# Diagonal tap weights on GpSimd, halved first projections and an earlier place for two scales in a fused Mamba-2 block

## The reference

```python
x = x + 0.5 * ffn(layernorm(x))        # W = (q - zeros) * scales, plus a rank 16 pair, plus bias
x = x + attn(layernorm(x))             # mamba2 block and a gated MLP
x = x + 0.5 * ffn(layernorm(x))

zxbcdt = rmsnorm(x) @ w_in.T           # z 512, xs 128, Bs 128, Cs 512, dt 4
xBC = silu(conv4(concat(xs, Bs, Cs)) + conv_b)      # causal, depthwise, 4 taps
# scan in chunks of 128 tokens, 4 heads; y = (Yd + Yo + D * xh) * silu(z)
h = x + y @ w_out.T
out = h + (silu(h2 @ gate_w.T) * (h2 @ up_w.T)) @ down_w.T     # h2 = rmsnorm(h), 1792 wide
```

## Time and profile before

| | |
|---|---|
| time, median of 3 | 753.17 us (751.98 to 754.31) |
| time of the profiled execution | 752.58 us |
| its span, first to last instruction | 750.8 us |
| PE busy | 737.4 us (98%) |
| DVE busy | 638.3 us (85%) |
| ACT busy | 456.5 us (61%) |
| POOL busy | 340.9 us (45%) |

### The profile page before, as it was taken

One profiled execution on the slowest core, in us unless ns is written; L12 is line 12 of the kernel. 1 busy time (PEld: TensorE's weight loads), 2 busy tenths in 40 slices (PEclk: granted clock), 3 DMA queues, 4 the chain that ended last, 5 costly groups with the idle time before them and its releaser, 6 DMA issues.

```text
span 750.8 us, 10655 instructions
## 1 busy us (share of the span) xinstructions
PE 737.4 (98%) x3424; PEld 359.9 (48%) x3424; DVE 638.3 (85%) x1257; ACT 456.5 (61%) x895; POOL 340.9 (45%) x391
## 2 busy tenths in 40 slices
PE   8999999999999999979999999999999999999998
PEld 3444455555555565534444444444444444444444
DVE  7799999899989997969899977977977978767994
ACT  4868888787787777435446456456356456444441
POOL 5631455665453357796323243243242242214574
PEclk9999999999999999999999999999999999999999
DMA  8933656574431233440612735634734733434464
GB/s 295 205 74 71 161 109 118 127 141 99 96 88 34 41 75 93 92 105 1 155 28 50 162 56 97 157 56 85 169 57 84 161 65 71 84 71 80 116 169 141
DMA packets 98790, 77.67 MB, mean 103 GB/s; under 512 B 65600, under 2 KB 73088, under 8 KB 98736
## 3 DMA queue, kind: packets, MB, share of 16 engines
q0 software_dynamic: 17280, 31.46, 23.6%
q1 hardware_dynamic: 78592, 41.01, 21.1%
q10 hardware_dynamic: 2864, 4.52, 2.2%
HBM read 24.77 MB, written 5.54 MB: 40 GB/s over the span
## 4 chain that ended last, share of the span: by engine, by line
PE 71%; DVE 17%; POOL 3%; issue 3%; ACT 3%; DMA 2%; ACTq 0%; POOLq 0%; DVEq 0%; SPq 0%
PE PS L2290 62%; DVE stage L1678 2%; DVE st L1500 1%; PE PS L2428 1%; DMA x_t<-hb 1%; PE PS L2420 1%; PE PS L2386 1%; DVE h2n_p L1591 1%; DVE raw L1678 1%; PE PS L2413 1%; PE PS L2404 1%; PE PS L2378 1%; PE PS L2417 1%; PE PS L2396 1%; DVE S L1635 1%
## 5 line engine op out<-in xcount | busy, mean ns | idle before, releaser
L2290 PE MATMUL PS<-h,w_in 128*128 128x512 f16 x480 | 108.1, 379 | 0.4 <-DMA h<-hn_p 0.4
L2290 PE MATMUL PS<-h,x_t 128*128 128x512 f16 x408 | 94.3, 380 | 0.6 <-DVE PS L2114 0.5
L785 POOL DMA_DIRECT2D xs<-x x42 | 36.7, 881 | 92.1 <-ACT x L1363 90.7
L2290 PE MATMUL PS<-n_T,stage 128*128 128x512 f16 x288 | 72.9, 384 | 3.9 <-DVEq L1732 3.9
L2290 PEld LDWEIGHTS PS<-h,w_in 128*128 128x128 f16 x480 | 46.4, 98 | 62.1 <-issue 11.1
L1363 ACT ACTIVATE x<-PS,d_d 128x512 f32<-128x512 f32 x59 | 40.3, 682 | 39.3 <-PE PS L2290 38.4
L2290 PEld LDWEIGHTS PS<-h,x_t 128*128 128x128 f16 x408 | 39.5, 98 | 49.2 <-issue 2.7
L586 POOL TENSOR_TENSOR r<-mv,mhalf 128x1 f32<-128x1 f32 (+1 forms) x32 | 29.1, 908 | 53.1 <-DVE mv L1504 38.4
L1333 ACT ACTIVATE xds<-tm,dgh 128x512 f32<-128x512 f32 x24 | 17.3, 722 | 53.2 <-DVE tm L2214 53.2
L2290 PE MATMUL PS<-pre,stage 128*128 128x512 f16 x192 | 49.3, 379 | 0.0
L2290 PEld LDWEIGHTS PS<-n_T,stage 128*128 128x128 f16 x288 | 28.3, 99 | 38.8 <-DVEq L1732 4.4
(11 more groups left out here) (349 smaller groups left out, 1882.4 us busy)
## 6 DMA issues: line engine op xcount, KB each, us to landing
xs<-x POOLq DMA_DIRECT2D x58, 256.0 KB, 3.3
xs<-n POOLq DMA_DIRECT2D x21, 256.0 KB, 3.3
xl<-x POOLq DMA_DIRECT2D x17, 256.0 KB, 3.3
x_t<-x_in SPq DMA_DIRECT2D x16, 256.0 KB, 3.5
x_t<-hb POOLq DMA_DIRECT2D x16, 256.0 KB, 4.7
out<-x_t SPq DMA_DIRECT2D x15, 256.0 KB, 2.3
raw_gu<-gate_t SPq DMA_DIRECT2D x7, 512.0 KB, 4.5
raw_gu<-up_t SPq DMA_DIRECT2D x7, 512.0 KB, 6.3
```

Of the source, the lines that this page charges most:

```text
L785: po.dma_start(end_row(c), d_tmps[d % 3], accum_op=ALU.add).then_inc(s_acc[d % 3], 16)
L2290: ins = pe.matmul(out_, lhs(a, b, k), rhs(a, b, k), start=first and n == 0, stop=last and n == len(todo) - 1)
```

## The change

At the start: POOL builds the twelve diagonal matrices instead of ACT, two at a time between its other work, and clears `hist`, `state` and `dA` instead of DVE; the first two wait for the loads of `s_head`. The small tables are padded to 32 rows on the host, so their four loads wait for no clearing and stand first in SP's queue; the bias load stands behind the q loads. ACT does `w_in_sum` sooner, `tc0(4)` behind `hi1(2, 2)`, and `w_in_hi` of piece 0 in front of `hi0(5, 1)`. DVE does `w_in_bound`, `max_row(1)` and `both_scales` each one step sooner. PE does projections 0 and 1 in halves of 256 tokens; the first halves stand around `first_t0(5)`, in front of `first_f(5)`. Three idle float32 matmuls are gone, and two of the nine junk ones.

At the end of the scan: DVE does `t_los(0, 1)` behind `gate_up(0, 3)`, and `t_los(1, 2)`, `gate_lo(0, 4)` and `lo2(15)` behind `gate_up(0, 4)` but in front of `scale_read(1)`; POOL does `rms2(15)` four sums sooner; ACT's list follows.

```diff
-N_WARM = 9
+N_WARM = 7
         for q in range(NPL):
-            put_proj(0, q)
+            if q < NPC:
+                PLAN["proj", 0, q] = B_CONV[q], (e_scale, 1)
+            else:
+                put_proj(0, q)
...
+            def build_dw(b, first):
+                for k in range(first, first + NTAP // 2):
+                    last = po.tensor_scalar(dw[:, b, k, :], ident[:, :], cw[:, b, k:k + 1], None, ALU.mult)
+                if first > 0:
+                    last.then_inc(e_dw, 1)
...
+            po.wait_ge(s_head, 48)
+            build_dw(0, 0)
             ln0(0, 0)
+            build_dw(0, 2)
...
             xb(1, 1)
+            build_dw(1, 0)
             ln0(3, 3)
+            build_dw(1, 2)
+            build_dw(2, 0)
             xb(2, 2)
+            build_dw(2, 2)
             ln1_chain(0, 0)
...
-                sums(8, 16)
+                sums(8, 12)
                 rms2(3 * CH + 3, 3)
-                sums(16, 20)
+                sums(12, 20)
...
-                t_his(1, 0, 1, 2, 3)
+                t_his(1, 0, 1)
...
+            gate_a(0, EARLY_GU)
+            t_his(1, 2)
             hi2(NCH - 1, CH - 1)
+            gate_b(0, EARLY_GU)
...
+            t_his(1, 3)
...
-                t_los(0, 1)
                 gate_up(0, 3)
                 residual2(c, 3)
                 gate_lo(0, 3)
-                t_los(0, 2, 3)
+                t_los(0, 1, 2, 3)
                 lo2(c - 1)
                 bound_row(1)
-                t_los(1, 0, 1, 2, 3)
-
+                t_los(1, 0, 1)
...
             gate_up(0, EARLY_GU)
+            t_los(1, 2)
+            gate_lo(0, EARLY_GU)
+            lo2(NCH - 1)
             scale_read(1)
             scales(1)
             descale(1)
-            gate_lo(0, EARLY_GU)
+            t_los(1, 3)
...
+            def proj_half(q, n):
+                b, freed = PLAN["proj", 0, q]
+                at, cols = DI + q * P, slice(n * (ST // 2), (n + 1) * (ST // 2))
...
             first_f(4)
+            proj_half(0, 0)
             first_t0(5)
+            proj_half(1, 0)
             first_f(5)
-            pe.wait_ge(e_zero, 2)
-            for _ in range(3):
-                pe.matmul(bank(B_SS), idle_r[:, 0:P], idle_r[:, :], start=True, stop=True)
```

More of the change, by code:

```diff
@@ L30, in build @@
 def build(nc, x_in, w_in_t, conv_w, conv_b, a_log, d_skip, dt_bias, w_out_t, ln1_w, ln2_w,
-          gate_t, up_t, down_t, q_t, scales_t, zeros_t, lora_a, lora_b_t, bias, out):
+          gate_t, up_t, down_t, q_t, scales_t, zeros_t, lora_a, lora_b_t, bias, out, RANK):
     T, DM = x_in.shape
@@ L640, in _ @@
             po.sem_inc(e_tab, 1)
+            for cleared in (hist[:, :, :], state[:, :, :], dA[:, :, :]):
+                chain(po.memset(cleared, 0.0))
+            po.wait_ge(s_head, 48)
+            build_dw(0, 0)
             ln0(0, 0)
+            build_dw(0, 2)
             chain(po.memset(tri[:, :], 1.0))
@@ L952, in taps_done @@
                 return (e_cv, n + 1) if n < NPC else (e_taps, n + 1 - NPC)
[L954 to L957, removed]
             def conv_pre(b):
@@ L2082, in _ @@
             x1_stats(1, 1, B_P[1])
+            w_in_bound()
             lo1(0, 0)
             prep0(4, 0)
+            max_row(1)
             x1_stats(2, 2, B_P[0])
-            w_in_bound()
             lo1(1, 1)
             prep0(5, 1)
-            max_row(1)
+            both_scales()
             x1_stats(3, 3, B_P[1])
-            both_scales()
             lo1(2, 2)
+            w_in_lo(0)
             lo1(3, 3)
-            w_in_lo(0)
             x1_stats(4, 0, B_P[0])
@@ L2125, in _ @@
             late_steps()
-            lo2(NCH - 1)
             def down(i):
@@ L2315, in proj @@
                 if q == 0:
-                    if i == 0:
-                        for c in range(CH):
-                            pe.wait_ge(s_h1[c], 16)
-                        pe.wait_ge(e_wlo, 1)
-                    else:
-                        pe.wait_ge(s_hT, i * CH * 16)
+                    pe.wait_ge(s_hT, i * CH * 16)
                 if i == 0 and q == CB:
@@ L2325, in proj @@
                 product(bank(b), lambda a, b, k: w_in[b][:, k, at:at + P], lambda a, b, k: h2T[a][:, k, tokens], KB).then_inc(e_proj, 1)
+            def proj_half(q, n):
+                b, freed = PLAN["proj", 0, q]
+                at, cols = DI + q * P, slice(n * (ST // 2), (n + 1) * (ST // 2))
+                if q == 0:
+                    for c in range(n * (CH // 2), (n + 1) * (CH // 2)):
+                        pe.wait_ge(s_h1[c], 16)
+                if n == 0:
+                    pe.wait_ge(e_wlo, 1)
+                    pe.wait_ge(*freed)
+                last = product(PS[:, b, cols], lambda a, b_, k: w_in[b_][:, k, at:at + P], lambda a, b_, k: h2T[a][:, k, cols], KB)
+                if n == 1:
+                    last.then_inc(e_proj, 1)
             def steps(i):
@@ L2734, in columns, with padded @@
         return np.asarray(v).reshape(-1, P).T
+    def padded(rows):
+        return np.concatenate([rows, np.zeros((QUAD - rows.shape[0], rows.shape[1]), rows.dtype)])
     arrays = {
@@ L2760 @@
     out = nc.dram_tensor("out", arrays["x_in"].shape, F32, kind="ExternalOutput").ap()
-    build(nc, out=out, **args)
+    build(nc, out=out, RANK=np.asarray(L0_ffn_lora_A).shape[0], **args)
     r = run_bass_kernel_spmd(nc, [arrays], core_ids=[0])
```

83 lines of the change are left out of this document (32 added, 51 removed).

## The result

The changed kernel took 759.03 us (median of 5, 757.18 to 759.18), the kernel before 754.18 us in the same comparison (5 runs): ratio 1.0064, 95% interval 1.005 to 1.0078. That is slower by 4.8 us, outside the range given. Its profiled execution has a span of 755.6 us, 4.8 more than the 750.8 of before, so the traces hold a difference of the same size. It is one of the two shorter executions (757.39 us at a mean clock of 0.995); the three of 759.0 to 759.2 us had 0.991 to 0.993. PE's busy time barely changed (736.9 us, before 737.4); what grew is its waits, and the stretches at the lower clock.

What follows compares the result with a forecast made beforehand. PE was taken as the bound, busy 737.4 of 750.8 us. Head +0.2 and end of the scan +0.7 gave +0.9: 753.5 us on the profiled execution's 752.58, 754.1 against the median, stated as 753.8, range 749.9 to 755.9.

Steps and rivals of the forecast that it cites:

- The head, +0.2 forecast: Start of the kernel up to `steps(0)`: net 0.2 us slower, with bounds of -1.7 and +1.5.
- So `ln0(0)` ends at 7.1 + 1.4 + 0.9 = 9.4: POOL's start: tap table lands at 7.1, two products take 1.4, `ln0(0)` 0.9, so it ends at 9.4 us.
- PE stands still for some 2 us there: PE ahead of its first transposes: idle some 2 us, transposing at 10.3 instead of 9.21, `first_f(0)` at 14.5.
- the rival of the falling clock: Rival: PE's 3.0 us stall ahead of `first_f(4)` lowers the clock, 1.7 us more, total 756.0 us; chance 0.14.
- the step on `tc0(4)`: Head: `tc0(4)` behind `hi1(2)` ends at 33.95, so `first_f(4)` starts 2.5 us later, PE idle about 3.0 us.
- has the 0.5 us at the mask in hand: Start of the scan: PE, 0.4 us late, can absorb that in its 0.5 us wait for POOL's decay mask.
- What is gained at the head by all engines together stays to the end: Mask to 311 us: PE hardly waits, so a gain at the head by all engines is kept in full.
- the rival in which the head keeps its gain: Rival: POOL's products hide, `steps(0)` comes at 44.7, the head gains 1.7 us, total 751.6 us; chance 0.16.
- The end of the scan, +0.7 forecast: Near 332 us: `e_wscale` comes at 332.8 instead of 332.16, 0.7 us slower, bounds -3.0 and +2.0.
- The bank's 0.5 us: Near 313 us: `gate_up(0, 3)` 0.6 us sooner on DVE removes PE's 0.5 us wait for a bank.
- POOL's wait for `t_los(0, 1)` is 6 us: End of the scan: POOL waits 6 us, before 3.67, for `t_los(0, 1)`; its sum starts at 314.7 instead of 312.08.
- The early scales: Rival: DVE runs unhindered, the 3.9 us scales wait becomes 2.4, clock stays up, 3.0 us saved, total 749.8; chance 0.22.

Runs made afterwards that it cites:

- e1: Changed kernel with its end of the scan written as in the kernel before, head still changed: ratio 1.0035, span 752.0 us.
- e4: Changed kernel with POOL's `ln0(0)` ahead of the tap table's wait and the first two products: ratio 1.0054, span 756.4 us.
- e13: e10 with POOL's second-panel weight sums (`s_adds(1)`) moved ahead of five sums of h2: ratio 0.994, median 748.87 us.
- e15: Head of the kernel before combined with e13's end of the scan: ratio 0.9946, median 748.95 us.
- e5: Changed kernel with PE waiting only for DVE's copy of the bounds out of the bank, not for the scales' end: ratio 1.0058, span 755.6 us.
- e9: e8's head with the end of the scan reordered anew on DVE, ACT and POOL: ratio 0.9984, median 751.40 us.
- e3: Changed kernel with `t_los(0, 1)` alone put back ahead of `gate_up(0, 3)`: ratio 1.0013, span 753.1 us.
- e8: e3 with `ln0(0)` first on POOL, tap products later on POOL, and `tc0(4)` ahead of `hi1(2)`: ratio 0.998, span 750.0 us.
- e6: Changed kernel with ACT's `tc0(4)` put back ahead of `hi1(2)`: ratio 1.0069, span 757.7 us.
- e7: Changed kernel with 16 junk matmuls on PE in the stall ahead of `first_t0(0)`: ratio 1.0062, span 756.3 us.
- e14: Changed kernel with POOL's `s_adds(1)` one sum sooner: ratio 1.0061, span 757.7 us.
- e10: e9 with `both_scales`, `w_in_lo(0)` and `w_in_hi(0)` sooner and `small_scales` behind `w_in_lo(1)` in the head: ratio 0.998, median 752.25 us.

## Why the prediction was wrong

**The head, +0.2 forecast, +2.44 measured.** It comes apart in four. The step that failed is the first, `first_f(0)`: forecast +0.1, measured +2.8. "So `ln0(0)` ends at 7.1 + 1.4 + 0.9 = 9.4" had the table land at 7.1, by the issue-to-landing time of the kernel before, though I wrote that the loads fill the DMA engines and the change puts others in front; it landed at 8.15. The products took 0.60 each, not 0.70. So the transposes came at 11.42, not 10.3, "PE stands still for some 2 us there" became 3.66, and the clock fell: from the transposes to `first_f(0)` it took 5.77 us, and 4.33 in e1, where the clock stayed up. I had the rival of the falling clock, with a price of 1.7 us (here 1.4), but tied it to the stall ahead of `first_f(4)` and did not ask it of this one. Nor did I ask when x would land behind the padded tables; without the table's wait that is what leaves 0.96 us of the stall in e4.

From `first_f(0)` to `first_f(4)`: forecast 19.5 us, measured 18.9, before 17.1. POOL's queue came as forecast (the first bias DMA at 14.90 for 14.4, `ln1_chain(0)` at 24.55 for 24.5), and the step on `tc0(4)` was right. Where the first stall is nearly away (e4) `first_f(4)` starts at 33.92, forecast 33.95, behind 3.31 us of stall, forecast 3.0, and the rival's clock is there as well. That it fits so closely is luck: in e4 `x1_stats(2)` starts at 28.17 and `hi1(2)` 3.7 us behind it, where I had 28.9 and 3.0. And in the changed kernel `x1_stats(2)` starts at 30.35, behind the two waits on ACT's last row sum that I left out.

From `first_f(4)` to `steps(0)`: forecast 12.95, measured 12.67, before 14.82; the halves and the dropped idle matmuls are worth the 2 us that I took. Last, I took off 0.4 us, as PE "has the 0.5 us at the mask in hand". Of the 2.5 us at `steps(0)` 2.44 arrived: POOL's mask came 2.5 us later too (its first select at 88.32, before 85.83), and the wait of 0.5 us stayed.

**"What is gained at the head by all engines together stays to the end"** holds for what is lost. A gain of 1.1 us at `steps(0)` was gone at 304 us (e13 against e15), 0.6 of it in the longer wait for the first masked S, which DVE and POOL brought no sooner. The first 0.7 us did arrive: e15 has the head of the kernel before, but its profiled execution ran `steps(0)` at 45.54 and not at 46.27, and was 0.8 us sooner at 304 us. So the rival in which the head keeps its gain could not have come true as priced.

**The end of the scan, +0.7 forecast, +2.37 measured.** The working up to the scales was near: POOL's sum behind `t_los(0, 1)` started at 317.37, on the old clock 314.93 (forecast 314.7), its wait was 6.5 us (6), and the scales' release came 1.1 us later than before (0.7). The bank's 0.5 us were gained and more was lost to the spread, as `bound_row(1)` stood behind a `t_los` and a `lo2` of 1.64 and 1.75 us beside POOL's sums; both vanish in the wait that DVE ends. The step that failed here is that the sum stopped at `e_wscale`. "POOL's wait for `t_los(0, 1)` is 6 us" stands there without its second consequence: all of POOL's queue, and with it the second panel's sums, come 5.2 us later, 2.8 beyond the head's delay, and PE met them 23 us behind the scales for 1.15 us more. e5, e9 and e13 show that this queue and the last transposition are what this place costs, as much as the scales.

**The sum.** 2.44 + 2.37 = 4.8 us, the difference of the traces. Of the 3.9 us that were missed, 2.2 are the head's (2.7 by the table's landing with the stall and the clock behind it, 0.4 by the mask's wait, less 0.5 and 0.3 at the other two), 0.4 the scales', and 1.3 the second panel's.

**The rivals.** The early scales, with the clock up, came true in e3 and in e8, which has the same end of the scan, and in e3 0.4 us arrived against before of the 3.0 that I had given them. In the changed kernel the wait was 4.0 us. The clock case was the right side and the right mechanism at the wrong stall.

## What to carry to other kernels

When an operation is moved behind a wait, follow the whole queue behind it to its last consumer, not to the next wait that the profile shows: here POOL's sums came due 23 us behind the last wait that I looked at. A wait on a semaphore names what PE stood for, not what would release it if that came sooner: take it away in a trial (e5) before building on it. Where work is moved to an idle engine, its place counts for more than its engine, and the first thing to price is whether its own input is there yet.

## What the runs showed of the hardware

In the profiled executions every stall of PE of 2.88 us and more was followed by a stretch at the lower clock (a granted clock of 0.50 to 0.58 in the 2 to 3 us behind it; behind the 3.89 us of e1 0.71, then 0.50), and so was one of 2.04 us (e6: 0.51) and, 1.4 us late, one of 2.06 (e9: 0.94, then 0.50). Stalls of 2.05 (e10), 2.15 (e3, e8), 2.53 and 2.70 (e1) and 2.66 us (e5) were not. A stall of 2.62 us was followed by it in e7 and e14 (eight matmuls in 5.40 and 6.63 us) and not in e3, e5 and the changed kernel (3.70). So among these shorter ones the length of the stall alone does not tell. The Trainium skill, TensorE: Matmul & The Clock Gate, section Why this matters for your kernels, advises against such gaps; the traces agree. One kernel takes several times: e1 took 753.8, 755.2 or 756.9 us at mean clocks of 0.998, 0.995 and 0.993. That its clock fell at the same stalls there is likely, but only one execution of it has a trace. The kernel before spreads as well (752.0 to 753.6, and 754.6 to 755.3 us, at one mean clock of 0.998); for that I have no cause.

A 128x128 product on POOL took 0.59 us in one place of the changed kernel and 0.75 in another, where I had taken 0.70 for all. And the time from a load's issue to its landing moved with the order of the other loads: the tap table took 3.7 to 4.4 us in the four profiled executions with the old head, and 4.8 to 5.9 in the thirteen with padded tables in front; DVE's first statistics of x began at 3.4 to 3.6 us in those, and at 5.7 to 6.6 in these. Which of the moved loads did it was not tested.
